# TensorE's depthwise taps as flat runs of 390 elements, with 20 more columns on the first of sixteen tiles

## The reference, cut to what matters

```
h = relu(bn1(conv1x1(x, w_pw1))) * mask_dilate      # 48 -> 288 channels
h = h * vector                                      # per image, 144 of the 288 channels are kept
h = relu(bnd(dwconv3x3(h, w_dw))) * mask            # depthwise 3x3, SAME padding
h = h * vector
h = bn2(conv1x1(h, w_pw2)) * mask                   # 288 -> 48
return x + h
```

## Time and profile before

| what | value |
|---|---|
| median of 3 runs | 1727.64 us (1726.21 to 1728.47) |
| span of the profiled execution | 1727.3 us |
| TensorE matmul busy | 1616.2 us, 94% |
| ScalarE busy | 1264.7 us, 73% |
| VectorE busy | 1192.9 us, 69% |

### The profile page before, as it was taken

The page is one execution under the profiler, slowest core; times in us unless marked ns, Lnnn a source line. Parts: engine busy times, 40 slices in busy tenths (PEclk is TensorE's granted clock), DMA queues, the critical chain, the costliest instruction groups (busy, mean ns, idle before and its releaser), DMA issues. The chain is left out here.

```text
span 1727.3 us, 57365 instructions
## 1 busy us (share of the span) xinstructions
PE 1616.2 (94%) x23474; PEld 1246.9 (72%) x23474; DVE 1192.9 (69%) x1989; ACT 1264.7 (73%) x2393; POOL 110.9 (6%) x189
## 2 busy tenths in 40 slices
PE   6999999999999999999999877467999999999996
PEld 6999999999999999999999832124444444444443
DVE  5777777777777777777777655775666666666664
ACT  5888888888888888888888844754665566565563
POOL 4000000000000000000000000000000000000000
PEclk9999999999999999999999989776999999999998
DMA  5666566566666666666666489840233333333334
GB/s 149 167 170 165 156 170 167 165 161 170 176 168 165 165 169 163 170 167 163 162 172 168 120 314 389 342 185 14 61 81 80 80 81 80 81 80 81 78 82 89
DMA packets 97151, 257.69 MB, mean 149 GB/s; under 512 B 23048, under 2 KB 29084, under 8 KB 96924
## 3 DMA queue, kind: packets, MB, share of 16 engines
q1 hardware_dynamic: 85496, 219.86, 43.7%
q0 software_dynamic: 10880, 35.40, 10.1%
q10 hardware_dynamic: 644, 0.49, 0.1%
HBM read 127.03 MB, written 85.08 MB: 123 GB/s over the span
## 5 line engine op out<-in xcount | busy, mean ns | idle before, releaser
L288 PE MATMUL gates<-state,w_high 64*128 64x384 f32 x4608 | 504.4, 337 | 0.0
L288 PEld LDWEIGHTS gates<-state,w_high 64*128 64x128 f32 x4608 | 416.5, 185 | 0.0
L1247 PE MATMUL psd<-shared 32*32 32x384 f32 x10368 | 296.8, 491 | 2.1 <-issue 1.0
L288 PE MATMUL gates<-state,w_low 64*128 64x384 f32 x2304 | 267.6, 337 | 0.0
L1247 PEld LDWEIGHTS psd<-shared 32*32 32x32 f32 x10368 | 161.9, 103 | 135.6 <-issue 81.6
L288 PE MATMUL gates<-x_both,w_high 64*128 64x384 f32 x2304 | 237.3, 338 | 13.7 <-ACT w_high L342 13.7
L347 ACT ACTIVATE sig_f<-gates 48x384 f32<-48x384 f32 x384 | 187.0, 487 | 48.0 <-PE gates L288 42.8
L288 PEld LDWEIGHTS gates<-x_both,w_high 64*128 64x128 f32 x2304 | 207.5, 186 | 13.7 <-ACT w_high L342 13.7
L288 PEld LDWEIGHTS gates<-state,w_low 64*128 64x128 f32 x2304 | 208.6, 185 | 0.0
L1485 DVE SCALAR_TENSOR_TENSOR acc<-shared,acc 128x768 f32<-128x768 f32 x144 | 146.5, 1018 | 81.7 <-ACT acc L1395 77.9
L1485 DVE SCALAR_TENSOR_TENSOR acc<-h,shared,acc 128x768 f32<-128x768 f32 x144 | 146.5, 1017 | 73.7 <-ACT acc L1395 69.8
(11 more groups left out here) (153 smaller groups left out, 1620.8 us busy)
## 6 DMA issues: line engine op xcount, KB each, us to landing
x_taps<-x_both SPq DMA_DIRECT2D x192, 195.5 KB, 3.3
x_raw<-x_steps SPq DMA_DIRECT2D x192, 192.0 KB, 3.2
h_rows<-h_new SPq DMA_DIRECT2D x168, 192.0 KB, 2.7
h_in<-h_rows SPq DMA_DIRECT2D x42, 768.0 KB, 6.3
x_last<-x_both SPq DMA_DIRECT2D x192, 98.0 KB, 3.0
shared<-x_parts SPq DMA_DIRECT2D x24, 768.0 KB, 9.3
out<-y SPq DMA_DIRECT2D x48, 336.0 KB, 5.5
out<-z POOLq DMA_DIRECT2D x47, 336.0 KB, 5.6
```

The source lines that it names most:

```text
L288: return nc.tensor.matmul(gates[p][d][:, m, 0:NH], w[own, n, m, :], moving[own], start=start, stop=stop)
L1247: mm = nc.tensor.matmul(psd[lane:lane + 32, 2 * x + i, 0:NH], wt[own, to:to + 32], h1p[2 * (s % 2) + x][own, dy + 4 * m:dy + 4 * m + 4, dx ...
```

## The change

Every tap matmul reads one flat run of `TAP_PX` = 3 * 98 + 96 = 390 elements of `h1` in place of four pieces of 96. The run passes over the two border elements between rows, so 6 of the 390 sums are of no use. The sums lie in PSUM at a pitch of 98 per row, and `relu2p` picks 96 of each 98. The first of the sixteen matmuls of each tap gets `LEAD` = 20 more columns, 410 in all, which nothing reads.

```
+    TAP_PX = 3 * WP + W
+    LEAD = 20
...
                                 to = W_DG + 32 * (9 * (2 * k + x) + tap)
+                                flat = h1p[2 * (s % 2) + x][:].rearrange("p r w -> p (r w)")
+                                at = (dy + 4 * m) * WP + dx
...
-                                        mm = nc.tensor.matmul(psd[lane:lane + 32, 2 * x + i, 0:NH], wt[own, to:to + 32],
-                                                              h1p[2 * (s % 2) + x][own, dy + 4 * m:dy + 4 * m + 4, dx:dx + W],
+                                        count = TAP_PX + (LEAD if (m, x, i, b) == (0, 0, 0, 0) else 0)
+                                        mm = nc.tensor.matmul(psd[lane:lane + 32, 2 * x + i, 0:count], wt[own, to:to + 32],
+                                                              flat[own, at:at + count],
                                                               start=(tap == 0), stop=(tap == 8), skip_group_check=True)
...
-                        last = nc.scalar.activation(h2p[(2 * s + x) % 3][:, i, :], psd[:, 2 * x + i, 0:NH], ACT.Relu,
+                        last = nc.scalar.activation(h2p[(2 * s + x) % 3][:, i, :].rearrange("p (r w) -> p r w", w=W),
+                                                    psd[:, 2 * x + i, 0:4 * WP].rearrange("p (r w) -> p r w", w=WP)[:, :, 0:W],
+                                                    ACT.Relu,
                                                     bias=wt[:, col + 1:col + 2], scale=wt[:, col:col + 1])
```

## The result

The changed kernel takes 1732.03 us (median of 20 runs) against 1728.28 us for the kernel before (20 runs). The ratio is 1.0026, with a 95% interval from 1.0017 to 1.0035: 2.9 to 6.0 us slower, 4.5 in the middle. The forecast was 6.0 us slower, at the upper end of that interval.

What follows compares the result with a forecast made beforehand. TensorE's end-to-end matmuls were taken to bound the kernel: 3.2 us for columns plus 2.8 for the lead, with 0 for flat reads and ScalarE, made 1727.6 + 6.0 = 1733.7 us. The range was 1728 to 1742, the forecast's own 1732 to 1736.

Steps and rivals of the forecast that it cites:

- TensorE bounds the stage: Bottleneck stage: TensorE is busy 99.8 of 100 us, running matmuls end to end, so a tap's cost sets the time.
- The columns, + 3.2 us: Tap matmuls: 390 for 384 columns cost 10 ns in each of 324 taps, + 3.2 us.
- The lead, + 2.8 us, once in a run: Twenty more columns on tile 0 cost 33 ns once in each of 84 runs of taps, + 2.8 us.
- The second sign of a limit: First tap behind L1226's 16 matmuls starts only 14 matmuls, behind L1217 16: what stood before still took up places.
- the limit: TensorE holds about one tap's instructions, places given back in order; the next tile is admitted 0.19 us after the oldest ends.
- The 14: Matmuls seen started in the first tap of the run behind L1226, against 16 in 0.11 us behind L1217.
- A flat read gains nothing: Tap operand read without row breaks: 491 ns with breaks against 495 without, so 0 us.
- ScalarE's read is free: 144 activations reading PSUM at a pitch of 98 cost 0, with a cover of 0.48 us before TensorE waits.
- The total: Whole kernel: 3.2 + 2.8 = + 6.0 us on 1727.6 us, giving 1733.7 us.
- The end of the second stall: Rival: the lead removes the third tap's second gap, tile 1 waiting for itself; - 19.9 us, to 1707.8 us; 12 in 100.
- The longest tile in every tap: Rival: each tap ends with its longest tile and costs 43 ns more, + 14.0 us, 1741.7 us; 8 in 100.
- The replay: Model of a run of taps from load, streaming and admission times, giving 2.70, 3.54, 4.39 and 5.23 us for three to six taps.

Runs made afterwards that it cites:

- the two with merged runs: Kernel before with pw1 moved ahead so two three-tap runs become one of six, in all chunks or all but chunk 0: ratios 0.9997 and 1.0004.

## Why the prediction was right

*TensorE bounds the stage.* Right: the 5.8 us by which the stage grew are the runs' 5.9 us, and TensorE's waits for other engines in the changed kernel are those of the earlier trace rows:

```profile
PE psd L1252 <- ACT shared L1430: 0.6, 1, 0.6
PE ps L1274 <- ACT h2p L1430: 0.3, 1, 0.3
```

*The columns, + 3.2 us.* Right to the resolution of the chain: 0.27 us in a chunk with them alone.

*The lead, + 2.8 us, once in a run.* Right: 0.22 us in a chunk, 2.6 us. With 120 columns it stayed once in a run. The reason that I gave was narrower than the truth. I let the second tap hang on tile 0 as such; the run with tile 4 long shows that another tile does as well, and the one with eight long tiles that the price can come in every tap.

*The second sign of a limit.* This reading was wrong, though the limit was right. The 14 came from a window laid too early. One that starts 5 ns later has 15, and the sixteenth matmul is there by 1531.57:

```profile
1531.44:1531.55 0.11, 0.10 (x15) 1.00 1.11 363
1531.56:1531.57 0.01, 0.01 (x16) 1.00 0.81 308
```

All sixteen started within about 0.12 us, against 0.10 in the other run. A tile short of a place would have come about 0.19 us late, and none did. The limit rests on the pauses of the earlier trace rows and on the experiments.

*A flat read gains nothing.* Right: 384 columns in a flat run give the same lengths. The rule that I had cited from the Trainium skill's page "PSUM — Partial Sum Buffer" says nothing against it, as the sums were contiguous in PSUM either way; for the operand in SBUF the runs show no price of a break after 96 elements (2.70 us for three taps with and without).

*ScalarE's read is free.* Right: 668 ns before and after.

*The total.* The six microseconds show as 5.9 in the profile's runs and as 4.5 (2.9 to 6.0) over the executions. Executions of one kernel lie up to 8.5 us apart (1728.07 to 1736.59), and the stalls without a releaser differ by up to 4.4 us between profiles, so the executions alone could not confirm the sum to better than about 1.5 us. That each term is right is shown by the lengths of the runs, and not by how near the forecast of 1733.7 us came to the median.

*The rivals.* The end of the second stall would have needed tile 1's pause to come from tile 1's own wait; the pause stayed with 20 and with 120 more columns. The longest tile in every tap is out by the 0.85 us of a further tap. The rule of the Trainium skill's "TensorE: Matmul & The Clock Gate" (measured speedup against the span model) is one matmul's duration plus about 4 ns for each further tile. It is for one bundle by itself, and no run here has such a bundle; the sixteen first passes of the earlier trace rows start about 7 ns apart, more than the page's 4. Read as a barrier behind each tap it gives the wrong price of a long tile, 0.89 us for a further tap in place of 0.85. The 64 entries of that page's table of specifications agree with the six-tap run at 14 tiles, 4.87 us, if each tile takes four of them.

## What to carry to other kernels

When many small tiles share the array, count the instructions in hand as well as the columns. A float32 tile has four in the profile, and sixteen of them, one tap, were all that TensorE held here. A tile that has ended gives its place back only after all before it, so lengthening one of them only holds up the rest: it cost 33 ns in a run with 20 more columns and 0.2 us with 120. To see this in a profile, cut the weight loads into windows of 0.1 us: a pause behind one early load is the sign, and a step in cost from run to run (0.84 against 0.64 us) its price.

## What the runs showed of the hardware that I had not expected

The replay has four constants: 27 ns from load to stream, 0.19 us from a tile's end to the next load, 16.6 ns between tiles in a refill and 6.6 ns between tiles in a run's first tap. With 0.194 for the 0.19 it meets the run lengths of nine kernels (all but the two with merged runs) within 10 ns, from 2.49 to 5.49 us; with 0.190 they come out up to 0.03 us short. The constants were read from the kernel before, so the other eight are tests of them. The places are given back in order: with a lead of 120 columns on tile 0, no load of the next tap's other tiles came before 0.19 us behind tile 0's end, though these tiles had streamed their columns at least 0.1 us earlier. And a tap with 12 tiles costs 0.645 us against 0.844 with 16, so 53.7 and 52.8 ns per tile: the last four tiles of a full array bring almost nothing once the places are used up.
